# First chunk of a fused block on Trainium2: first tiles centred on VectorE and scaled on ScalarE, weights by single blocks, first up blocks by token halves

## The chip, the cores and the metric

One core of one Trainium2 chip runs the kernel. The metric is the device time of one execution in microseconds; the number that counts is the median of several executions. TensorE (PE in the profile, with its weight loads as PEld), VectorE (DVE), ScalarE (ACT), GpSimd (POOL) and the queue of SyncE (SP, its transfers as SPq) each work through their own list in program order, and meet only through semaphores.

## What is computed

For 8192 rows `x` of 256 numbers, everything in float32:

```
xn  = layernorm(x)                                   # no weights
D   = clip(slope of the counts over the first 1024 numbers of xn, 1, 2)
x1  = real(ifft(fft(xn) * filter(D)))                # a 256x256 circulant
cor = golay_correct(x1 @ W_el + b_el > 0) @ W_le + b_le
ffn = gelu(xn @ w1 + b1) @ w2 + b2                   # 256 -> 1024 -> 256
out = x + x1 + cor + ffn
```

## The kernel before

**Tiles.** The rows are cut into 16 chunks of 512 tokens. In a chunk the feed-forward part is 8 *up* blocks of 128 hidden units (line 964) and 8 *down* blocks (lines 982, 987). Each float32 operand is split into a high part that TensorE reads at full rate and a rest, so every product is three: high x high, low x high, high x low. An up block is thus 6 matmuls of 512 columns into one of the two PSUM banks `p_h[:, m % 2]`; ScalarE turns it into `h` by Gelu (line 446), then into `h_hi` (line 454), and VectorE makes `h_lo` (line 633). An up block `m` may start when the Gelu of block `m - 2` has emptied its bank (`gelu_done`), and the Gelu of block `m` wants `h_lo` of block `m - 2` (`h_lo_done`).

**Start.** SyncE loads the four row tiles of chunk 0 in three pieces (first tile, second tile, last two), then the identity matrix for transposes, the weights `w1` in pieces of 2, 2 and 4 blocks with other inputs between, and so on. VectorE takes the statistics of two tiles at a time (lines 824 and 830), GpSimd makes the inverse root (line 361, `rstd_done`), VectorE normalises with subtract and multiply in one instruction (line 817), TensorE transposes four 128x128 blocks for two tiles (line 1139, into one bank of `p_s`), ScalarE copies that bank to `xT_hi` (line 518, `t0_hi`), and VectorE makes `xT_lo` (line 839, `t0_lo`). Ahead of all this TensorE does 12 matmuls on zeros (line 1132). The parts of `w1` are copied to `w1_hi` by ScalarE (line 507) and to `w1_lo` by VectorE (line 804).

**Order in chunk 0.** It is written out by hand on each engine. TensorE: the transposes of both halves; up block 0 by token halves (256 columns) and up blocks 1 to 3 whole; then down and up in turn, with three small sums over partitions for `D` (line 1126), the circulant (line 1110, after down 5) and the latent weights (line 1119, after down 6) between. The sum that gives `D` (`logged` to `dim_made`) stands after down 1. From it VectorE makes `angle` (lines 880 to 883), GpSimd runs 12 small instructions up to `filt_w` (line 395), and ScalarE makes `basis_w` (line 549), which the circulant reads. ScalarE's list at the start:

```
w1_part_hi(0)
for g in range(2):
    act.wait_ge(t0_done, g + 1)
    nc.scalar.copy(half_tokens(xT_hi[0], g), half_bank(g)).then_inc(t0_hi, 1)
w1_part_hi(1)
act.wait_ge(small_in, 16)
gelu(0, 0, first=True)
hidden_hi(0, 0, first=True)
w2_part_hi(0)
gelu(0, 1, first=True)
```

**Later chunks** run one pattern, in a loop over pairs of chunks. The change leaves them alone.

Of the kernel before, what the change touches and what calls it, by code (L numbers as in the profile page):

```python
# [7 lines left out]
ALU = mybir.AluOpType  # L8
# [3 lines left out]
P = 128  # L12
TOKENS, E, HID, LAT, SYN = 2 * 4096, 256, 1024, 24, 12
TILES = TOKENS // P
CT = 4
CTOK = CT * P
# [6 lines left out]
W1_PARTS = ((0, 2), (2, 4), (4, 6), (6, MB))  # L23
W1_LOADS = ((0, 2), (2, 4), (4, MB))
# [40 lines left out]
def build(nc, x, xt, small, latent, w1, w2, ident, consts, basis, out):  # L65
    ctx = ExitStack()
    with ctx:
# [109 lines left out]
        id_in, con_in, basis_in, small_in = sem("id_in"), sem("con_in"), sem("basis_in"), sem("small_in")  # L177
# [13 lines left out]
        xn0_done, t0_done, t0_hi, t0_lo = sem("xn0_done"), sem("t0_done"), sem("t0_hi"), sem("t0_lo")  # L191
# [52 lines left out]
        def _(sp):  # L244
# [163 lines left out]
        def _(act):  # L408
# [117 lines left out]
            w1_part_hi(2)  # L526
# [3 lines left out]
            w1_part_hi(3)  # L530
# [46 lines left out]
        def _(dve):  # L577
# [235 lines left out]
            def normalise(g):  # L813

                dve.wait_ge(rstd_done, g + 1)
                for j in range(g * HALF, (g + 1) * HALF):
                    last = nc.vector.tensor_scalar(xn0[:, j, :], x_sb[0][:, j, :], mv[0][:, j, 0:1],  # L817
                                                   row_nums[0][:, 1, j:j + 1], ALU.subtract, ALU.mult)
                last.then_inc(xn0_done, 1)


# [5 lines left out]
            aggregate(0, range(HALF))  # L827
            dve.wait_ge(x_in[0], 16)
# [19 lines left out]
            w1_part_lo(1)  # L848
# [26 lines left out]
            w1_part_lo(3)  # L875
# [60 lines left out]
        def _(pe):  # L936
            mm = nc.tensor.matmul

            def up(c, par, m, first=False):

                if m == 0 and not first:

                    pe.wait_ge(t_lo, c)
                for n, (m0, _) in enumerate(W1_PARTS):
                    if first and m == m0:

                        pe.wait_ge(*((w1_hi_ready, 1) if n == 0 else (w1_ready, n + 1)))
                if not (first and m < 2):

                    pe.wait_ge(gelu_done, MB * c + m - 1)  # L950

                groups = 2 if first and m == 0 else 1
                for g in range(groups):
                    tok = slice(g * CTOK // groups, (g + 1) * CTOK // groups)
                    n = 0
                    for w, xp in ((w1_hi, xT_hi), (w1_lo, xT_hi), (w1_hi, xT_lo)):
                        if groups == 2:

                            if w is w1_lo and g == 0:
                                pe.wait_ge(w1_ready, 1)  # L960
                            elif w is w1_hi:
                                pe.wait_ge(t0_hi if xp is xT_hi else t0_lo, g + 1)
                        for k in range(KB):
                            last = mm(p_h[:, m % 2, tok], w[:, k, m * P:(m + 1) * P], xp[par][:, k, tok],  # L964
                                      start=(n == 0), stop=(n == 3 * KB - 1))
                            n += 1
                last.then_inc(up_done, 1)
# [165 lines left out]
            pe.wait_ge(id_in, 16)  # L1133
            for g in range(2):

                pe.wait_ge(xn0_done, g + 1)
                for k in range(KB):
                    for j in range(HALF):
                        last = nc.tensor.transpose(half_bank(g)[:, k, j * P:(j + 1) * P],  # L1139
                                                   xn0[:, g * HALF + j, k * P:(k + 1) * P], id_sb[:])  # L1140
                last.then_inc(t0_done, 1)

            pe.wait_ge(pool_set, 3)
            for m in range(LOOK):
# [3 lines left out]
            for m in range(MB):  # L1148
# [3 lines left out]
                if m == 1:  # L1152
# [16 lines left out]
def constants():  # L1169
# [50 lines left out]
    return np.eye(P, dtype=f4), con, basis  # L1220
# [47 lines left out]
```

## Time and profile before

| what | value |
|---|---|
| median of 3 runs | 407.75 us (407.51 to 407.8) |
| the profiled execution | 407.3 us, of which the span of the trace is 405.5 us |
| busy in the span | PE 99%, PEld 81%, DVE 74%, ACT 55%, POOL 21% |
| granted TensorE clock | 1.0 of full in every slice |
| chain that ended last | 97% PE |

The span runs from the first to the last instruction of the trace, and 1.8 us of the execution lie around it. All positions below are microseconds from the start of the span. A matmul's busy time contains its pipeline, so the pace of TensorE is read from the starts of the weight loads, which follow one another without overlap of their starts.

### The profile page before, as it was taken

What the parts mean: (1) busy time and instruction counts of PE and PEld (TensorE: products, weight loads), DVE (VectorE), ACT (ScalarE), POOL (GpSimd) and SP (SyncE); (2) the same over time, 40 slices, a digit from 0 to 9 for tenths busy, and PEclk for the clock granted to TensorE, in tenths of its full rate; (3) what the DMA queues carried; (4) which work ended last, traced back from release to release, by engine and by line L of the source; (5) the groups of instructions that cost most, each with busy time, mean ns of one, the idle gap of its engine ahead of it and who ended that gap; (6) DMA issues with size and microseconds to landing.
All of it is one profiled execution on the core that took longest, in us unless ns stands there. A gap on an engine that the chain in (4) does not pass through costs nothing.

```text
span 405.5 us, 5548 instructions
## 1 busy us (share of the span) xinstructions
PE 400.7 (99%) x1774; PEld 329.1 (81%) x1774; DVE 298.7 (74%) x512; ACT 223.3 (55%) x333; POOL 87.2 (21%) x102
## 2 busy tenths in 40 slices
PE   8999999999999999999999999999999999999997
PEld 3888888888888888888888888888888888888886
DVE  5879985878658795677957788476974868757656
ACT  3967556557354664537545474554736556365561
POOL 3142421313003131121313013131121312113000
PEclk9999999999999999999999999999999999999999
DMA  6554333213333213333123332023333031111011
GB/s 187 218 158 156 104 103 106 63 42 104 103 104 98 44 65 103 104 103 97 46 64 104 103 104 90 26 91 103 104 103 78 40 89 53 54 52 52 2 52 52
DMA packets 15307, 35.75 MB, mean 88 GB/s; under 512 B 5440, under 2 KB 6592, under 8 KB 15296
## 3 DMA queue, kind: packets, MB, share of 16 engines
q1 hardware_dynamic: 15152, 35.49, 27.4%
q10 hardware_dynamic: 144, 0.13, 0.1%
q8 instruction: 5, 0.08, 0.1%
q14 instruction: 6, 0.05, 0.0%
HBM read 27.17 MB, written 8.45 MB: 88 GB/s over the span
## 4 chain that ended last, share of the span: by engine, by line
PE 97%; DMA 1%; DVE 1%; POOL 0%; SPq 0%; issue 0%
PE p_h L964 43%; PE p_f L982 28%; PE p_f L987 14%; PE p_s L1030 5%; PE p_l L1017 4%; PE p_s L1038 2%; DMA x_sb<-x 1%; PE p_f L997 0%; SPq L248 0%; DVE stats L830 0%; POOL row_nums L361 0%; DVE rows_sb L817 0%; PE p_g L1006 0%; PE p_l L1006 0%; PE p_s L1139 0%
## 5 line engine op out<-in xcount | busy, mean ns | idle before, releaser
L446 ACT ACTIVATE h<-p_h,small_sb 128x512 f32<-128x512 f32 x128 | 88.2, 689 | 139.4 <-PE p_h L964 138.9
L633 DVE TENSOR_TENSOR h_lo<-h,h_hi 128x512 fp32r<-128x512 f32 x128 | 102.9, 804 | 69.2 <-ACT h_hi L454 69.2
L982 PE MATMUL p_f<-h_hi,w_hi 128*128 128x512 f32 x252 | 98.3, 390 | 0.0
L982 PE MATMUL p_f<-h_hi,w_lo 128*128 128x512 f32 x252 | 98.1, 389 | 0.0
L369 POOL TENSOR_TENSOR uv<-xn 128x512 f32<-128x512 f32 x30 | 59.3, 1996 | 126.0 <-DVE xn L618 126.0
L454 ACT CAST h_hi<-h 128x512 fp32r<-128x512 f32 x128 | 79.5, 621 | 5.8
L964 PE MATMUL p_h<-xT_hi,w_hi 128*128 128x512 f32 (+1 forms) x258 | 79.4, 389 | 0.0
L964 PE MATMUL p_h<-xT_lo,w_hi 128*128 128x512 f32 (+1 forms) x258 | 79.2, 388 | 0.0
L964 PE MATMUL p_h<-xT_hi,w_lo 128*128 128x512 f32 (+1 forms) x258 | 79.0, 387 | 0.0
L987 PE MATMUL p_f<-h_lo,w_hi 128*128 128x512 f32 x252 | 77.6, 389 | 0.0
L964 PEld LDWEIGHTS p_h<-xT_lo,w_hi 128*128 128x128 f32 x258 | 48.3, 188 | 10.3 <-DVE xT_lo L839 0.2
L964 PEld LDWEIGHTS p_h<-xT_hi,w_lo 128*128 128x128 f32 x258 | 48.3, 188 | 9.9
L964 PEld LDWEIGHTS p_h<-xT_hi,w_hi 128*128 128x128 f32 x258 | 48.0, 188 | 9.6
L982 PEld LDWEIGHTS p_f<-h_hi,w_hi 128*128 128x128 f32 x252 | 47.3, 188 | 10.0 <-issue 0.2
L987 PEld LDWEIGHTS p_f<-h_lo,w_hi 128*128 128x128 f32 x252 | 47.3, 188 | 9.9
L982 PEld LDWEIGHTS p_f<-h_hi,w_lo 128*128 128x128 f32 x252 | 47.3, 188 | 9.7
L356 POOL TENSOR_TENSOR var_eps<-mv,eps 128x4 f32<-128x4 f32 (+1 forms) x17 | 3.9, 227 | 153.3 <-DVE mv L596 153.3
L676 DVE SCALAR_TENSOR_TENSOR xt_sb<-p_f,bias,xt_sb 128x512 f32 (+1 forms) x30 | 21.1, 745 | 11.7 <-PE p_f L987 11.7
L416 ACT CAST xT_hi<-xn 128x1024 fp32r<-128x1024 f32 x15 | 15.8, 1054 | 19.8 <-DVE xn L618 19.8
L613 DVE TENSOR_TENSOR xn<-xt_sb,rows_sb 128x1024 f32<-128x1024 f32 x15 | 18.4, 1224 | 11.0 <-DMA rows_sb<-rows_dram 11.0
L628 DVE TENSOR_TENSOR uv_lo<-uv,uv_hi 128x1024 fp32r<-128x1024 f32 x16 | 19.3, 1203 | 3.3 <-ACT uv_hi L423 3.3
L591 DVE BATCH_NORM_STATS2 stats<-x_sb 128x6 f32<-128x256 f32 x60 | 21.0, 412 | 0.0
(127 smaller groups left out, 325.2 us busy)
## 6 DMA issues: line engine op xcount, KB each, us to landing
xt_sb<-xt SPq DMA_DIRECT2D x16, 512.0 KB, 5.3
x_sb<-x SPq DMA_DIRECT2D x15, 512.0 KB, 4.6
rows_sb<-rows_dram SPq DMA_DIRECT2D x15, 512.0 KB, 4.4
out<-xt_sb SPq DMA_DIRECT2D x15, 512.0 KB, 2.8
xt_sb<-w SPq DMA_DIRECT2D x3, 512.0 KB, 7.5
xt_sb<-w SPq DMA_DIRECT2D x2, 256.0 KB, 4.5
x_sb<-x SPq DMA_DIRECT2D x2, 128.0 KB, 2.1
x_sb<-x SPq DMA_DIRECT2D x1, 256.0 KB, 3.2
```

The lines of the kernel that those rows point to most:

```text
L369: nc.gpsimd.tensor_tensor(uv[:, k, :], xn[:, 0, :], xn[:, 1, :], op).then_inc(turned, 1)
L446: nc.scalar.activation(h[m % 2][:], p_h[:, m % 2, :], ACT.Gelu, bias=small_sb[:, S_B1 + m:S_B1 + m + 1]).then_inc(gelu_done, 1)
L454: nc.scalar.copy(h_hi[m % HR][:], h[m % 2][:]).then_inc(h_hi_done, 1)
L591: last = nc.vector.bn_stats(stats[:, j, :], x_sb[par][:, j, :])
L613: nc.vector.tensor_tensor(xn[:, :, :], columns(c), to_halves(rows_sb[par][:, 0, :]), ALU.subtract).then_inc(centred, 1)
L628: nc.vector.tensor_tensor(uv_lo[:, :, :], uv[:, :, :], uv_hi[:, :, :].bitcast(F32), ALU.subtract).then_inc(u_lo, 1)
L633: nc.vector.tensor_tensor(h_lo[m % HR][:], h[m % 2][:], h_hi[m % HR][:].bitcast(F32), ALU.subtract).then_inc(h_lo_done, 1)
L676: nc.vector.scalar_tensor_tensor(out=xc, in0=p_f[:, k, :], scalar=bias[:, k:k + 1], in1=xc, op0=ALU.add, op1=ALU.add).then_inc(ffn_added, 1)
L964: last = mm(p_h[:, m % 2, tok], w[:, k, m * P:(m + 1) * P], xp[par][:, k, tok], start=(n == 0), stop=(n == 3 * KB - 1))
L982: mm(p_f[:, a, :], w[:, m, a * HF:(a + 1) * HF], h_hi[r][:], start=(m == 0 and w is w2_hi), stop=False, skip_group_check=True)
L987: last = mm(p_f[:, a, :], w2_hi[:, m, a * HF:(a + 1) * HF], h_lo[r][:], start=False, stop=(m == MB - 1), skip_group_check=True)
L1030: last = mm(p_s[:, k, :], w[:, k, :], xp[:, k, :], start=(n == 0), stop=False, skip_group_check=True)
```

## The change

The identity matrix is no longer loaded: GpSimd makes it from `ones` with one affine_select, ahead of its four zeroing memsets. `w1` arrives and is split in parts of 1, 1, 2, 2 and 2 blocks (loads of 1, 1, 2 and 4). For the first two tiles VectorE only subtracts the mean, before it takes the statistics of the other two, and ScalarE multiplies by the inverse root. TensorE transposes tile by tile instead of column half by column half. Up blocks 0 and 1 are both done by token halves, in both banks of `p_h` at once; their first products for the first half stand ahead of the transposes of the second half. `up_done`, which releases the Gelu of blocks 0 and 1, comes with the last two pairs of matmuls. On VectorE the statistics of chunk 1 go ahead of `h_lo` of block 1; on TensorE the sum that gives `D` goes from behind down 1 to behind down 2.

```diff
-W1_PARTS = ((0, 2), (2, 4), (4, 6), (6, MB))
-W1_LOADS = ((0, 2), (2, 4), (4, MB))
+W1_PARTS = ((0, 1), (1, 2), (2, 4), (4, 6), (6, MB))
+W1_LOADS = ((0, 1), (1, 2), (2, 4), (4, MB))
...
-            sp.dma_start(id_sb[:], ident).then_inc(id_in, 16)
+            sp.dma_start(small_sb[:], small).then_inc(small_in, 16)
             load_w1(0)
-            sp.dma_start(small_sb[:], small).then_inc(small_in, 16)
             load_w1(1)
+            load_w1(2)
             sp.dma_start(con[:], consts).then_inc(con_in, 16)
             load_w2(0)
             load_x(1)
-            load_w1(2)
+            load_w1(3)
...
+            pool.wait_ge(pool_set, 3)
+
+            nc.gpsimd.affine_select(out=id_sb[:], in_=ones[:], pattern=[[1, P]], base=0, channel_multiplier=-1,
+                                    compare_op=ALU.is_equal, fill=0.0).then_inc(id_made, 1)
             for q in range(2):
                 nc.gpsimd.memset(cw[q][:].bitcast(F32), 0.0).then_inc(cw_set, 1)
                 nc.gpsimd.memset(le2[q][:].bitcast(F32), 0.0).then_inc(le_set, 1)
-            pool.wait_ge(pool_set, 3)
...
+            act.wait_ge(rstd_done, 1)
+            for j in range(HALF):
+                act.wait_ge(centred0, j + 1)
+                nc.scalar.mul(xn0[:, j, :], xn0[:, j, :], row_nums[0][:, 1, j:j + 1]).then_inc(scaled0, 1)
             w1_part_hi(0)
+            w1_part_hi(1)
             for g in range(2):
                 act.wait_ge(t0_done, g + 1)
                 nc.scalar.copy(half_tokens(xT_hi[0], g), half_bank(g)).then_inc(t0_hi, 1)
-            w1_part_hi(1)
+            w1_part_hi(2)
...
+            dve.wait_ge(stat_done, 1)
+            for j in range(HALF):
+                nc.vector.tensor_scalar(xn0[:, j, :], x_sb[0][:, j, :], mv[0][:, j, 0:1], None,
+                                        ALU.subtract).then_inc(centred0, 1)
             dve.wait_ge(x_in[0], 16)
             for j in range(HALF, CT):
                 last = nc.vector.bn_stats(stats[:, j, :], x_sb[0][:, j, :])
             last.then_inc(stats_made, 1)
             dve.wait_ge(stats_made, 2)
             aggregate(0, range(HALF, CT))
-            for g in range(2):
-                normalise(g)
             w1_part_lo(0)
+            dve.wait_ge(rstd_done, 2)
+            for j in range(HALF, CT):
+                nc.vector.tensor_scalar(xn0[:, j, :], x_sb[0][:, j, :], mv[0][:, j, 0:1], row_nums[0][:, 1, j:j + 1],
+                                        ALU.subtract, ALU.mult).then_inc(xn0_done, 1)
             for g in range(2):
                 dve.wait_ge(t0_hi, g + 1)
...
+                if g == 0:
+                    w1_part_lo(1)
...
-            w1_part_lo(2)
-            hidden_lo(0, 1)
+            w1_part_lo(3)
             statistics(1, 1)
             dve.wait_ge(stats_made, 3)
             aggregate(1)
+            hidden_lo(0, 1)
             hidden_lo(0, 2)
...
+            def first_ups():
+
+                turn_rows(0, scaled0)
+                pe.wait_ge(t0_hi, 1)
+                for m in range(2):
+                    pe.wait_ge(w1_hi_ready, m + 1)
+                    half_up(m, 0, (0,))
+                turn_rows(1, xn0_done)
+                pe.wait_ge(w1_ready, 1)
+                half_up(0, 0, (1,))
+                pe.wait_ge(t0_lo, 1)
+                half_up(0, 0, (2,))
+                half_up(1, 0, (2,), last_term=1)
+                pe.wait_ge(w1_ready, 2)
+                half_up(1, 0, (1,), last_term=1)
+                pe.wait_ge(t0_hi, 2)
+                half_up(0, 1, (0, 1))
+                half_up(1, 1, (0, 1))
+                pe.wait_ge(t0_lo, 2)
+                half_up(0, 1, (2,)).then_inc(up_done, 1)
+                half_up(1, 1, (2,)).then_inc(up_done, 1)
...
-            for m in range(LOOK):
+            first_ups()
+            for m in range(2, LOOK):
                 up(0, 0, m, first=True)
...
-                if m == 1:
+                if m == 2:
                     summed_over(16, 1, fr_d[:, 0:1], logged, dim_made)
```

`half_up(m, g, terms)` issues, for each of its terms (0 high x high, 1 low x high, 2 high x low), two matmuls of 256 columns into token half `g` of bank `m`. `turn_rows(g, ready)` issues four transposes, two for each tile as the tile becomes ready. Up block 2 still waits for the Gelu of block 0, and up block 3 for that of block 1.

## Rows read from the trace of the kernel before

**Rows 1.** The page, busy time, share of the span and number of instructions by engine.
```profile
PE 400.7 (99%) x1774; PEld 329.1 (81%) x1774; DVE 298.7 (74%) x512; ACT 223.3 (55%) x333; POOL 87.2 (21%) x102
```

**Rows 2.** Timeline, 0 to 8.6 us: start, length, engine, line, operation, [idle before].
```profile
1.19 5.30 PE L1132 MATMUL p_f<-idle 128*128 128x512 bf16 x12 [1.19 <-DVE idle L578]
4.42 0.71 POOL L361 TENSOR_TENSOR row_nums<-var_eps,minus_half 128x2 f32<-128x2 f32 x1
...
6.62 0.42 PEld L1139 LDWEIGHTS p_s<-id_sb,rows_sb 128*128 128x128 f32 x4 [1.04 <-issue]
...
7.09 0.62 ACT L507 CAST w_hi<-xt_sb 128x512 fp32r<-128x512 f32 x1 [4.86 <-DMA xt_sb<-w]
...
7.62 0.58 ACT L518 CAST xT_hi<-p_s 128x512 fp32r<-128x512 f32 x1
...
7.89 0.66 PE L1139 MATMUL p_s<-id_sb,rows_sb 128*128 128x128 f32 x4 [0.61 <-DVE rows_sb L817]
...
8.31 0.30 PEld L964 LDWEIGHTS p_h<-xT_hi,w_hi 128*128 128x128 f32 x2
...
8.59 0.59 ACT L518 CAST xT_hi<-p_s 128x512 fp32r<-128x512 f32 x1 [0.39 <-PE p_s L1139]
```

**Rows 3.** Timeline, 9.3 to 13.2 us, the up blocks 0 to 3 and their Gelus.
```profile
9.32 0.30 PEld L964 LDWEIGHTS p_h<-xT_hi,w_hi 128*128 128x128 f32 x2
...
9.55 0.30 PEld L964 LDWEIGHTS p_h<-xT_hi,w_lo 128*128 128x128 f32 x2
...
9.95 0.30 PEld L964 LDWEIGHTS p_h<-xT_lo,w_hi 128*128 128x128 f32 x2
...
10.56 0.69 ACT L446 ACTIVATE h<-p_h,small_sb 128x512 f32<-128x512 f32 x1 [0.87 <-PE p_h L964]
...
11.46 0.41 PEld L964 LDWEIGHTS p_h<-xT_hi,w_hi 128*128 128x128 f32 x2
...
12.33 0.68 ACT L446 ACTIVATE h<-p_h,small_sb 128x512 f32<-128x512 f32 x1
...
13.16 0.30 PEld L964 LDWEIGHTS p_h<-xT_hi,w_hi 128*128 128x128 f32 x2
```

**Rows 4.** DMA issues of the first 30 us: KB each, median us to landing.
```profile
xt_sb<-w SPq DMA_DIRECT2D x2, 256.0 KB, 4.5
...
x_sb<-x SPq DMA_DIRECT2D x2, 128.0 KB, 2.1
...
small_sb<-small SPq DMA_DIRECT2D x1, 30.0 KB, 4.2
```

**Rows 5.** ScalarE by form, first 35 us: busy us, mean ns.
```profile
L556 ACT ACTIVATE le_h<-le_t 128x256 fp32r<-128x256 f32 x1 | 0.4, 427 | 0.0
```

**Rows 6.** Timeline, GpSimd at the start.
```profile
0.80 0.20 POOL L339 MEMSET ones<- 128x128 f32 x1
...
4.15 0.20 POOL L356 TENSOR_TENSOR var_eps<-mv,eps 128x2 f32<-128x2 f32 x1 [2.15 <-DVE mv L596]
```

**Rows 7.** The page, GpSimd's costliest group: busy, mean ns, idle before.
```profile
L369 POOL TENSOR_TENSOR uv<-xn 128x512 f32<-128x512 f32 x30 | 59.3, 1996 | 126.0 <-DVE xn L618 126.0
```

**Rows 8.** Timeline, the chain from the sum for D to the circulant.
```profile
18.79 0.42 PEld L1126 LDWEIGHTS p_g<-fr_d,ones 128*128 128x128 f32 x2
...
20.31 0.15 DVE L880 TENSOR_SCALAR fr_d<-p_g 128x1 f32<-128x1 f32 x1
...
26.01 0.19 POOL L395 TENSOR_TENSOR filt_w<-series 128x2 f32<-128x2 f32 x1
...
27.50 0.69 ACT L549 ACTIVATE basis_w<-basis_sb,filt_w 128x128 f32<-128x128 f32 x2
...
28.55 0.65 PEld L1110 LDWEIGHTS p_l<-basis_w,basis_sb 128*128 128x128 f32 x4
```

**Rows 9.** Timeline, the statistics of chunk 1 and the Gelu of block 3.
```profile
15.42 1.40 DVE L591 BATCH_NORM_STATS2 stats<-x_sb 128x6 f32<-128x256 f32 x4
...
16.37 0.68 ACT L446 ACTIVATE h<-p_h,small_sb 128x512 f32<-128x512 f32 x1
```

More of the change, by code:

```diff
@@ L62, with build @@
 S_END = S_WEL + KB * LAT
-def build(nc, x, xt, small, latent, w1, w2, ident, consts, basis, out):
+def build(nc, x, xt, small, latent, w1, w2, consts, basis, out):
     ctx = ExitStack()
@@ L176, in build @@
         w2_in = [sem(f"w2_in{i}") for i in range(len(W2_LOADS))]
-        id_in, con_in, basis_in, small_in = sem("id_in"), sem("con_in"), sem("basis_in"), sem("small_in")
+        id_made, con_in, basis_in, small_in = sem("id_made"), sem("con_in"), sem("basis_in"), sem("small_in")
         latent_in, stored = sem("latent_in"), sem("stored")
@@ L190, in build @@
         veps_done, rstd_done, mean_done = sem("veps_done"), sem("rstd_done"), sem("mean_done")
[L191 removed]
+        centred0, scaled0, xn0_done, t0_done, t0_hi, t0_lo = sem("centred0"), sem("scaled0"), sem("xn0_done"), sem("t0_done"), sem("t0_hi"), sem("t0_lo")
         fr_taken, xc0_made = sem("fr_taken"), sem("xc0_made")
@@ L525, in _ @@
             hidden_hi(0, 1, first=True)
-            w1_part_hi(2)
+            w1_part_hi(3)
             gelu(0, 2, first=True)
@@ L529, in _ @@
             w2_part_hi(1)
-            w1_part_hi(3)
+            w1_part_hi(4)
             gelu(0, 3, first=True)
@@ L811, in w2_part_lo @@
                                         ALU.subtract).then_inc(w2_ready, 1)
[L813 to L819, printed above, removed]
             for j in range(HALF):
@@ L847, in _ @@
             values = fr_v[:, :].unsqueeze(1).broadcast_to(table)
-            w1_part_lo(1)
+            w1_part_lo(2)
             first_rows = p_s[:, :, :].rearrange("p g (a t) -> p (g a) t", t=P)[:, :, 0]
@@ L874, in _ @@
                                     ALU.add).then_inc(logged, 1)
-            w1_part_lo(3)
+            w1_part_lo(4)
             w2_part_lo(1)
@@ L945, in up @@
                     if first and m == m0:
[L947 to L966, printed above, removed]
@@ L967, in up @@
-                last.then_inc(up_done, 1)
+                        pe.wait_ge(w1_ready, n + 1)
+                pe.wait_ge(gelu_done, MB * c + m - 1)
+                n = 0
+                for w, xp in ((w1_hi, xT_hi), (w1_lo, xT_hi), (w1_hi, xT_lo)):
+                    for k in range(KB):
+                        last = mm(p_h[:, m % 2, :], w[:, k, m * P:(m + 1) * P], xp[par][:, k, :],
+                                  start=(n == 0), stop=(n == 3 * KB - 1))
+                        n += 1
@@ new lines, in up, with turn_rows, half_up @@
+                last.then_inc(up_done, 1)
+            def turn_rows(g, ready):
+                for j in range(HALF):
+                    pe.wait_ge(ready, j + 1)
+                    for k in range(KB):
+                        last = nc.tensor.transpose(half_bank(g)[:, k, j * P:(j + 1) * P],
+                                                   xn0[:, g * HALF + j, k * P:(k + 1) * P], id_sb[:])
+                last.then_inc(t0_done, 1)
+            def half_up(m, g, terms, last_term=2):
+                tok = slice(g * GTOK, (g + 1) * GTOK)
+                for n in terms:
+                    w, xp = ((w1_hi, xT_hi), (w1_lo, xT_hi), (w1_hi, xT_lo))[n]
+                    for k in range(KB):
+                        last = mm(p_h[:, m, tok], w[:, k, m * P:(m + 1) * P], xp[0][:, k, tok],
+                                  start=(n == 0 and k == 0), stop=(n == last_term and k == KB - 1), skip_group_check=True)
+                return last
@@ L1132, in _ @@
                 mm(p_f[:, 0, :], idle[:, 0:P], idle[:], start=True, stop=True)
[L1133 to L1141, printed above, removed]
+            pe.wait_ge(id_made, 1)
             pe.wait_ge(pool_set, 3)
-            for m in range(LOOK):
+            first_ups()
+            for m in range(2, LOOK):
                 up(0, 0, m, first=True)
@@ L1219, in constants @@
     assert a.sum(axis=1).min() >= 4
-    return np.eye(P, dtype=f4), con, basis
+    return con, basis
 def layouts(inputs):
@@ L1255 @@
     arrays = {name: np.ascontiguousarray(a) for name, a in layouts(inputs).items()}
-    for name, a in zip(("ident", "consts", "basis"), constants()):
+    for name, a in zip(("consts", "basis"), constants()):
         arrays[name] = a
```

## The prediction

> **What bounds the kernel now.** I read the page first. TensorE is busy in 99% of the span and no other engine in more than 81% [rows 1], and the chain that ended last runs over TensorE for 97% of it. So the time is what TensorE has to do plus the time in which it can't go on, and the change takes no real work from it: the same products, some of them in pieces of 256 columns. What can move is the head, so I then read the timeline of the first 15 us, engine by engine, and there the starts of the weight loads, because a matmul's busy time hides small gaps.
>
> The head before reads like this. TensorE's matmuls on zeros end at 6.49 [rows 2]. The first transposes start at 6.62; ScalarE could take them at about 7.3, but it is on the first piece of `w1`, which landed at 7.09, and copies `xT_hi` from 7.62 to 8.20. The first up matmul loads at 8.31 [rows 2]. From there pairs of 256 columns go at 0.23 us a pair (9.32 to 9.55), so the six pairs of block 0 need 1.38; the last pair loads at 9.95, so they took until 10.18, and 0.49 of it was waiting for `xT_lo` and the second half [rows 3]. Then TensorE goes on without a pause: block 2 loads at 11.46, block 3 at 13.16, one block and one small sum (1.70) later [rows 3]. The Gelu of block 0 runs 10.56 to 11.25, so its bank is free just before block 2 wants it at 11.46; the Gelu of block 1 ends at 13.01, again just before 13.16 [rows 3]. After this I find no wait of TensorE worth counting in the first 40 us. The measure for the change is therefore one number: when blocks 2 and 3 load, against 11.46 and 13.16. I call the shift of block 3 **s**.
>
> **When the first up matmul loads (T).** Three things can set it.
>
> - *The rows.* The inverse root is there at 5.13 [rows 2]. The two subtractions fit into VectorE's pause before the second statistics, and cost nothing there. ScalarE waits for nothing else then, and its scaling of 128x256 is nearest to an ACTIVATE of that shape, 0.43 [rows 5]; two, overlapping, or at worst one after the other, end between 5.9 and 6.1.
> - *The matmuls on zeros* are in front of the transposes in TensorE's list and unchanged. The last ends at 6.49 with its pipeline; the next load may overlap it a little, so the transposes start at 6.3 to 6.5 instead of 6.62. In the second half ScalarE's copy began 0.70 after the transposes (7.89 to 8.59) [rows 2], so this path lets the copy begin at 7.0 to 7.2.
> - *The weights.* ScalarE now has parts 0 and 1 of `w1` ahead of this copy. The two are the bytes of the old first piece, but in two transfers; the first keeps its place in SyncE's list, the second is issued 0.47 later, in the place in which the small inputs were. The old piece took 4.5 from issue to landing, the small inputs 4.2, the first row tile, with an empty queue, 2.1 [rows 4]. The old issue was thus at 2.59 and the second one's is near 3.06; it lands between 5.2 (2.1 later) and 7.3 (4.2 later). With half the bytes of the old piece and the identity's 64 KB gone from ahead of it, I take 6.8, nearer to the late end, since what lies in front of it in the queue is the same. Half a copy (about 0.27, as 7.09 to 7.62 is 0.53 for the whole) brings the copy of `xT_hi` to 7.07.
>
> Both last paths meet near 7.1. Then 0.58 for the copy and 0.11 to the load, as from 7.62 to 8.31: T = 7.8, with 7.7 and 8.3 as ends. That is 0.5 earlier than before, and it is what the change gains.
>
> **What follows T.** Four half matmuls (0.46), then the second half's transposes. Their loads took 0.42 for the first half, and they were already through before T in the old order, so this is work that goes from a pause of TensorE into its busy time. The second copy of `xT_hi` begins 0.46 + 0.70 after T and is seen at T + 1.85. Until then TensorE has 0.46 + 0.44 + four pairs (0.92) = 1.82: no pause. VectorE has the two `xT_lo` in time: the first runs from about T to T + 0.7 and is wanted at T + 1.13, the second ends near T + 2.5 and is wanted at T + 2.77. The parts of `w1_lo` lie between them, with 0.4 or more to spare. So both blocks are issued at T + 0.46 + 0.44 + 10 pairs (2.30) = T + 3.2. With T = 7.8 this is 11.0, where the old order needed until about 11.5. So far 0.5 gained.
>
> **Where the gain goes.** Blocks 0 and 1 now end together. `up_done` comes first with the last but one pair, which loads at T + 2.77. Before, the Gelu of block 0 started 0.61 after the load of that block's last pair (9.95 to 10.56) [rows 3]. So it starts at T + 3.38 = 11.18, lasts 0.69, and block 2, which waits for it to empty the bank, loads 0.10 later, at T + 4.17 = 11.97. TensorE stands for 0.95 us, where it stood for nothing. Block 2 loads at 11.97 instead of 11.46: 0.5 late. For block 3 the Gelu of block 1 counts. Between the two Gelus ScalarE has `h_hi` of block 0 and a part of `w2`, 1.77 from start to start (10.56 to 12.33) [rows 3], and no idle time, so it starts at T + 5.15 and ends at T + 5.83, and block 3 loads at T + 5.94 = 13.74. By TensorE's own path it would be 11.97 + 1.70 = 13.67. Against 13.16 this is s = T - 7.22 = **+0.58**, from +0.48 (T = 7.7) to +1.08 (T = 8.3).
>
> **The rest of chunk 0.** The whole order moves by s; I looked for places where it moves by more.
>
> - *Statistics of chunk 1 ahead of `h_lo` of block 1.* Four instructions of 1.40 in all and four small ones [rows 9], with the second ones I count 1.8. Behind that `h_lo` waits the Gelu of block 3, at 16.37 before [rows 9]; it now starts near 17.9 and ends at 18.6. It is needed by up block 5, which now loads in the old place of the sum, 18.79 + s [rows 8]. The Gelu of block 4, behind three copies on ScalarE, ends near 21.7; it is needed by up block 6, two blocks (2.72) and a sum (0.34) after block 5, 21.8 + s. Costs 0, with 0.6 to spare; without that cover up to 0.9 us.
> - *The sum for D, one up and one down block later.* It loads at 21.5 + s instead of 18.79, but VectorE got to its result only at 20.31 [rows 8] and will at 22.1 + s, 1.8 later. So `filt_w` moves from 26.20 to 28.0 + s, and `basis_w` from 27.50 to 28.05 + s. Each of its two halves takes some 0.35; the circulant loads at 28.55 + s [rows 8] and its second half 0.28 later. They are ready at 28.4 and 28.75. It just fits: 0 to 0.1. Here VectorE and ScalarE stand in line behind the wait (`w2_lo`, `h_lo` of blocks 4 and 5, the Gelus of 6 and 7), but each of these is needed over 1 us later than it then comes.
> - *GpSimd.* No row shows an affine_select. Below it is bounded by the 128x128 memset, 0.20, above by a two-input operation on four times the elements, 2.0 [rows 6, 7]. GpSimd was idle for 2.15 before its first statistics at 4.15 [rows 6], so both ends cost nothing. I take 0.5. The identity is wanted at 6.3.
> - *One transfer less* (identity) saves nothing on the path beyond what stands above.
>
> The sum: -0.5 for the earlier start, +0.44 for transposes that move into busy time, -0.49 for the pauses of block 0 that go, +0.95 for the new pause, and some 0.15 where block 3 is held by ScalarE and in rounding: +0.55 to +0.6. The profiled execution was 407.3, its span 405.5, so I expect 407.9 for a profiled one; on the median of the runs, 407.75, it gives **408.35**.
>
> **One rule against the trace.** GpSimd's instructions of the start, each the first of its kind, took 0.1 to 0.7 us, the longest the power at 4.42 [rows 2, 6]. The Trainium skill (GPSIMD Engine Reference, Instruction dispatch) says that the first call of a freshly loaded kernel pays about 6 us to bring in its code. By that page, if it held for affine_select, the result would be near 411; the trace shows no such pause for the other operations.
>
> **The rivals.**
>
> 1. *Weights land late.* Two transfers, each with its own finish, land at 7.3 or after; T is 8.3 or more and s = +1.1, time 408.85. For it: the small inputs issued in that slot took 4.2 [rows 4]. Against it: less lies in the queue ahead.
> 2. *The chain for D loses its cover.* If the sum's result comes 0.5 later than I think, the circulant waits as long and everything behind it: s = +1.1 to +1.6, time 409.1. For it: 0.1 us of slack.
> 3. *The first copy is early enough (the other side).* It decides at T = 7.22. If the zeros ended by 6.0 and the weights landed by 6.1, the copy would begin at 6.4, T = 7.1 and s = -0.1; at T = 6.4, which needs the rows' path to end at 5.7, it would be 0.8 faster, 406.95. Against it: the 12 matmuls on zeros end at 6.49 and are not touched [rows 2]. The new pause can vanish too, if the next bank is seen free sooner than by the rows: then 407.4.
> 4. *GpSimd's first affine_select is slow.* It delays the first inverse root one for one beyond 2.15. A stall of 6 us in its place would put T near 11 and the time at 411.3.
> 5. *Nothing changes*: gain and pause cancel within 0.2, 407.75.
>
> **How the numbers follow.** The forecast (s from 0.4 to 0.8) has 0.55, the late weights 0.13, the lost cover 0.09, the other side 0.09, the slow affine_select 0.03, no change 0.11. A difference of 0.2%, 0.8 us, is about what a measurement of this kernel can tell from none. Of the forecast's own chance a tenth lies above 0.8, and of the first two rivals nearly all; of the other side half is faster by more than 0.2%. So slower 0.30, same 0.65, faster 0.05. The range, 407.5 to 409.1, leaves out the slow affine_select, the far part of the lost cover and most of the other side, together under 0.2; the forecast's own is 408.15 to 408.55.
>
> **What would show it.** In the profile after: transposes from 6.3 to 6.5 and the first up load at 7.7 to 8.3 (right), TensorE without a pause up to about 11, then one of 0.8 to 1.0 before block 2 that ends with the Gelu of block 0; block 3 near 13.75; the circulant near 29.15. The prediction is wrong if that pause is absent or small, if the first load is before 7.2 or after 8.6, if affine_select is longer than 2.1, or if there is a second pause between 16 and 32 us.

## The result, and the profile after

The changed kernel takes 409.81 us (median of 6 runs), the kernel before 407.59 on the same chips. The ratio is 1.0056, with a 95% interval of 1.0043 to 1.0069: 2.2 to 2.3 us slower. The forecast was 408.35 with a range to 409.1. Its account of the head held, and a second loss of 2 us was missed. Its point lay on the right side, though its chances did not favour it: "slower" had 0.30 and "same" 0.65. The missed loss is a pause between 16 and 32 us, which the prediction had named as a sign of being wrong.

First the page of the changed kernel: busy time by engine, and the chain that ended last.

```profile
span 407.9 us, 5566 instructions
...
PE 400.2 (98%) x1780; PEld 329.3 (81%) x1780; DVE 298.7 (73%) x513; ACT 224.2 (55%) x336; POOL 90.0 (22%) x103
...
PE 95%; POOL 2%; DMA 1%; ACT 1%; SPq 0%; issue 0%; DVE 0%; ACTq 0%
```

Against [rows 1] TensorE's busy time is the same within 0.5 us, and the span is 2.4 us longer, so the difference is TensorE standing. GpSimd has 2.8 us more busy time for one instruction more, and it now has 2% of the chain. Both are the trace of what follows.

The timeline of the head, the lines that answer to [rows 2, 3]:

```profile
6.07 0.54 PEld L972 LDWEIGHTS p_s<-id_sb,rows_sb 128*128 128x128 f32 x4 [0.98 <-issue]
...
6.52 0.71 ACT L510 CAST w_hi<-xt_sb 128x256 fp32r<-128x256 f32 x2 [0.17 <-DMA xt_sb<-w]
...
7.14 0.58 ACT L526 CAST xT_hi<-p_s 128x512 fp32r<-128x512 f32 x1
...
7.77 0.53 PEld L982 LDWEIGHTS p_h<-xT_hi,w_hi 128*128 128x128 f32 x4 [1.16 <-ACT xT_hi L526]
...
10.59 0.55 PEld L982 LDWEIGHTS p_h<-xT_lo,w_hi 128*128 128x128 f32 x4
...
11.21 0.69 ACT L449 ACTIVATE h<-p_h,small_sb 128x512 f32<-128x512 f32 x1 [1.11 <-PE p_h L982]
...
12.01 0.30 PEld L962 LDWEIGHTS p_h<-xT_hi,w_hi 128*128 128x128 f32 x2 [0.87 <-issue]
...
13.71 0.30 PEld L962 LDWEIGHTS p_h<-xT_hi,w_hi 128*128 128x128 f32 x2
```

The first up matmul loads at 7.77 (8.31 before), block 2 at 12.01 (11.46), after a pause of 0.87 that ends with the Gelu of block 0, and block 3 at 13.71 (13.16). The head is 0.54 us ahead at its start and 0.55 behind at its end.

Now the second loss. The waits of the weight loads in the first 60 us (us in total, times, longest), of which only this one stands behind block 3:

```profile
PEld p_l L1149 <- ACT basis_w L557: 2.0, 1, 2.0
```

And the timeline of what the circulant waited for, to be read against [rows 8]:

```profile
22.64 0.16 DVE L888 TENSOR_SCALAR fr_d<-p_g 128x1 f32<-128x1 f32 x1 [1.61 <-PE p_g L1165]
...
26.75 0.53 POOL L394 TENSOR_TENSOR halves<-halves,quads 128x8 f32<-128x8 f32 x1
27.36 1.06 POOL L395 TENSOR_TENSOR series<-halves,powers 128x4 f32<-128x4 f32 x1
28.49 1.19 POOL L396 TENSOR_TENSOR series<-series,halves 128x4 f32<-128x4 f32 x1
29.76 0.52 POOL L397 TENSOR_TENSOR series<-series,weighted 128x4 f32<-128x4 f32 x1
30.36 0.19 POOL L398 TENSOR_TENSOR filt_w<-series 128x2 f32<-128x2 f32 x1
...
31.09 0.59 PEld L1149 LDWEIGHTS p_l<-basis_w,basis_sb 128*128 128x128 f32 x4 [2.00 <-ACT basis_w L557]
```

VectorE reads the sum at 22.64, as forecast (22.1 + s). But `filt_w` is ready at 30.55 and not at 28.6: the GpSimd chain from `angle` on took 7.2 us, where it took 5.2 before. Beside the slow instructions VectorE did this:

```profile
25.93 1.29 DVE L641 TENSOR_TENSOR h_lo<-h,h_hi 128x512 fp32r<-128x512 f32 x2
27.14 1.22 DVE L621 TENSOR_TENSOR xn<-xt_sb,rows_sb 128x1024 f32<-128x1024 f32 x1
28.39 1.23 DVE L626 TENSOR_TENSOR xn<-xn,rows_sb 128x1024 f32<-128x1024 f32 x1
29.54 0.68 DVE L641 TENSOR_TENSOR h_lo<-h,h_hi 128x512 fp32r<-128x512 f32 x1
```

Put the ends side by side: VectorE's four end at 27.22 (the second of the two), 28.36, 29.62 and 30.22; GpSimd's four slow ones at 27.28, 28.42, 29.68 and 30.28. Each GpSimd instruction on four or eight numbers ends 0.06 us after a VectorE instruction with two operands in SBUF. So it looks as if it had not been working that long but standing; the third experiment tests that.

### The profile page after: what moved, and what is told of

The parts are those of the page before. It is cut to its first block, busy times and chain, and to the rows that moved or that the text cites. A ratio compares the mean times of both kernels' runs of the same rounds, so it can differ in the third digit from the quotient of the medians.

```text
span 407.9 us, 5566 instructions
## 1 busy us (share of the span) xinstructions
PE 400.2 (98%) x1780; PEld 329.3 (81%) x1780; DVE 298.7 (73%) x513; ACT 224.2 (55%) x336; POOL 90.0 (22%) x103
## 4 chain that ended last, share of the span: by engine, by line
PE 95%; POOL 2%; DMA 1%; ACT 1%; SPq 0%; issue 0%; DVE 0%; ACTq 0%
PE p_h L962 42%; PE p_f L1021 27%; PE p_f L1026 14%; PE p_s L1069 5%; PE p_l L1056 4%; PE p_s L1077 2%; DMA xt_sb<-w 1%; PE p_h L982 1%; PE p_f L1036 0%; SPq L248 0%; POOL series L396 0%; POOL powers L385 0%; POOL series L395 0%; PE p_l L1149 0%; PE p_g L1045 0%
## 5 line engine op out<-in xcount | busy, mean ns | idle before, releaser
L962 PE MATMUL p_h<-xT_hi,w_hi 128*128 128x512 f32 x252 | 78.0, 391 | 0.7 <-ACT h L449 0.7
L962 PE MATMUL p_h<-xT_lo,w_hi 128*128 128x512 f32 x252 | 77.6, 389 | 0.0
L962 PE MATMUL p_h<-xT_hi,w_lo 128*128 128x512 f32 x252 | 77.6, 389 | 0.0
L962 PEld LDWEIGHTS p_h<-xT_hi,w_hi 128*128 128x128 f32 x252 | 47.0, 188 | 10.4 <-issue 0.9
L962 PEld LDWEIGHTS p_h<-xT_lo,w_hi 128*128 128x128 f32 x252 | 47.3, 188 | 9.9
L962 PEld LDWEIGHTS p_h<-xT_hi,w_lo 128*128 128x128 f32 x252 | 47.3, 188 | 9.9
L684 DVE SCALAR_TENSOR_TENSOR xt_sb<-p_f,bias,xt_sb 128x512 f32 (+1 forms) x30 | 21.1, 746 | 11.9 <-PE p_f L1026 11.7
```

The costliest lines, as they stand in the source:

```text
L684: nc.vector.scalar_tensor_tensor(out=xc, in0=p_f[:, k, :], scalar=bias[:, k:k + 1], in1=xc, op0=ALU.add, op1=ALU.add).then_inc(ffn_added, 1)
L962: last = mm(p_h[:, m % 2, :], w[:, k, m * P:(m + 1) * P], xp[par][:, k, :], start=(n == 0), stop=(n == 3 * KB - 1))
```

## The experiments

All times are given against runs of the kernel before on the same chip, as a ratio with its 95% interval; its median there was 407.2 to 407.3 us.

**The sum back in its place.** Only this is undone in the changed kernel:

```diff
-                if m == 2:
+                if m == 1:
                     summed_over(16, 1, fr_d[:, 0:1], logged, dim_made)
```

> The changed kernel with one thing undone: the sum that gives D stands again behind down block 1 on TensorE. Theory A (the moved sum costs the 2.0 us pause ahead of the circulant, since the twelve GpSimd instructions start later and also run beside VectorE's centring and scaling of chunk 1): the chain on GpSimd starts near 21.5 and takes 5 to 5.5 us, the pause before the circulant is gone, and only the shift of the head, +0.55, is left: 0.5 to 0.7 us above the kernel before, about 1.7 us below the changed one. Theory B (the late VectorE and ScalarE order, with the statistics of chunk 1 ahead of h_lo of block 1, causes the pause; the sum's place is not what matters): the pause stays over 1 us and the time stays within 0.5 us of the changed kernel.

Measured 407.83, ratio 1.0026 (1.0013 to 1.004), by medians 0.6 us above the kernel before. The chain starts at 21.29 and ends at 26.45, and nothing waits for `basis_w` any more. Theory A holds, B falls. One thing was not expected, a new wait of 0.58 us ahead of the latent weights:

```profile
PEld p_g L1158 <- ACT c_f L561: 0.6, 1, 0.6
```

What sets this wait shows when the traces are laid side by side. VectorE starts to centre chunk 1 when its row numbers arrive, and the latent weights' product loads 3.88 or 3.89 us after that start, in the kernel before (26.54 and 30.43), here (27.29 and 31.17) and in all five kernels below that have a wait for `c_f`. The start is 0.75 us later here: the row numbers leave 0.14 later, and the rest is that their transfers took longer in this execution.

**The sum alone,** moved in the kernel before (`if m == 1:` to `if m == 2:`).

> The kernel before with only the sum for D moved behind down block 2. Theory A: the sum is read at about 22.05 instead of 20.31, the GpSimd chain starts near 22.7, its last four instructions fall beside VectorE's centring and scaling from 26.5 on and are stretched as in the changed kernel; filt_w is ready near 29.7 instead of 26.2, and TensorE pauses 1.5 to 2.2 us before the circulant: 1.3 to 2.0 us above the kernel before. Theory C (the GpSimd instructions merely vary from run to run; the move costs the slack of 1.8 minus 1.7): 0 to 0.4 us above.

Measured 409.04, ratio 1.0046 (1.0033 to 1.0059): 1.8 us above, from one moved matmul pair, and the wait for `basis_w` is 2.0. Its GpSimd rows repeat those of the changed kernel at other times (1.06, 1.18 and 0.52 us from 26.64, 27.77 and 29.04, under VectorE's centring, scaling and `h_lo` from 26.42), so this is no scatter. Theory C falls.

**VectorE stands aside.** The changed kernel, with one wait more:

```diff
             hidden_lo(0, 6)
+            dve.wait_ge(filt_made, 1)
             centre(1, 1)
```

> The changed kernel, with VectorE waiting for filt_w before it centres chunk 1, so that no two-input VectorE instruction runs beside the end of the GpSimd chain. Theory A: the last four GpSimd instructions (0.53, 1.06, 1.19 and 0.52 us in the changed kernel) shrink to 0.2 each, or 0.7 where something else ran beside them before; the chain ends near 28.5 instead of 30.55; the pause before the circulant falls from 2.0 to under 0.3, and a new one of up to 1 us may come further on, since centring now starts later: 0.5 to 1.8 us below the changed kernel. Theory C: their durations stay, and the time rises by 1 us or more, since centring waits.

Measured 409.17, ratio 1.0047 (1.0033 to 1.0062). By medians this is 0.6 us below the changed kernel, but each against the kernel before on its own chips they are 1.95 and 2.22 us slower, and the intervals overlap: a gain in time is not shown. What the experiment shows is in the timeline, the same instructions:

```profile
26.72 0.53 POOL L394 TENSOR_TENSOR halves<-halves,quads 128x8 f32<-128x8 f32 x1
27.32 0.20 POOL L395 TENSOR_TENSOR series<-halves,powers 128x4 f32<-128x4 f32 x1
27.60 0.20 POOL L396 TENSOR_TENSOR series<-series,halves 128x4 f32<-128x4 f32 x1
27.88 0.20 POOL L397 TENSOR_TENSOR series<-series,weighted 128x4 f32<-128x4 f32 x1
28.16 0.19 POOL L398 TENSOR_TENSOR filt_w<-series 128x2 f32<-128x2 f32 x1
```

1.06, 1.19 and 0.52 have become 0.20 each; the first, still beside an `h_lo`, stays at 0.53. `filt_w` is ready 2.2 us earlier although the chain began at the same time, and the circulant doesn't wait. The time does not fall by as much because centring is now late, at 28.38, and behind it `xT_hi` and `c_f`, for which the latent weights wait 1.4 (up to 1 us was expected).

**Half of the move,** the sum behind up block 5, in the kernel before and in the changed one (the call goes behind `up(0, 0, m + LOOK, first=True)` with `if m == 1:`).

> The kernel before with the sum for D one up block later than before, behind up block 5: half of the move of the change. Theory A (a threshold: the sum costs nothing until the GpSimd chain slides under VectorE's centring of chunk 1): VectorE reads the sum near 20.7, the chain ends between 26.6 and 27.5, the circulant does not wait, and the time is within 0.2 us of the kernel before. Rival G (the cost grows with the distance moved, 1.8 us for two places): 0.6 to 1.2 us above the kernel before.

Measured 407.37, ratio 1.0000 (0.9991 to 1.0008). No cost in the median, but the two other marks of theory A failed: in the profiled execution (407.59) the row numbers of chunk 1 arrived early, VectorE centred from 25.34, and the chain was stretched to 28.48, 7.3 us long, with 0.7 of wait before the circulant. Part of that came back, since the 0.2 us of wait before chunk 1's first down block were gone; the block loads at 39.91, 0.24 later than in the kernel before. So the place is at the edge, not safe: what the chain meets depends on when the row numbers arrive.

> The changed kernel with the sum for D behind up block 5 instead of behind down block 2. Theory A: no wait before the circulant beyond 0.3 us, time within 0.3 us of e1_sum_back, so 0.3 to 0.9 us above the kernel before. Rival G: half of the 2 us pause stays, 1.3 us or more above the kernel before.

Measured 408.12, ratio 1.0013 (1.0004 to 1.0022). The chain took 5.1 us and the circulant didn't wait; the wait for `c_f` was 1.1, with centring from 27.89. On the time theory A holds in both kernels and rival G falls; that the circulant doesn't wait holds here only. What counts is not how far the sum moves but what the chain then meets.

**The head alone,** with the statistics of chunk 1 behind `h_lo` of block 1 again and the sum back:

```diff
             w1_part_lo(3)
+            hidden_lo(0, 1)
             statistics(1, 1)
             dve.wait_ge(stats_made, 3)
             aggregate(1)
-            hidden_lo(0, 1)
```

> The changed kernel with both moves behind the head undone: the sum for D and the statistics of chunk 1 in their old places. What is left is the head alone (centring, scaling, single blocks, token halves, identity from GpSimd). Theory A: block 2 loads 4.2 us after the first up matmul, the wait for c_f is 0 to 0.6, and the time is 0.3 to 0.7 us above the kernel before. Rival F (the statistics' move helps, since the row numbers of chunk 1 leave earlier): e1_sum_back is faster than this by 0.2 us or more.

Measured 408.01, ratio 1.0017 (1.0002 to 1.0033), and 0.2 us of median apart from the kernel with only the sum back, whose interval overlaps. First up matmul 7.93, block 2 at 12.16: 4.23 apart, as in the changed kernel (4.24) and with the sum back (4.21). Whether the statistics' move helps is not told apart by this pair's times. The traces say how much it could: in the five kernels with the statistics in the place of the change the row numbers leave 11.7 us after the first up matmul loads, in the four with the old place 11.9 to 12.0.

**Where the 0.6 us near 30 comes from.** The statistics still earlier, in the time in which VectorE had nothing to do:

```diff
             nc.vector.tensor_reduce(fr_s[:, 0, :], fr_a[:], AX.X, ALU.add).then_inc(part_sums, 1)
+            statistics(1, 1)
+            dve.wait_ge(stats_made, 3)
+            aggregate(1)
             hidden_lo(0, 0)
...
             w1_part_lo(3)
-            statistics(1, 1)
-            dve.wait_ge(stats_made, 3)
-            aggregate(1)
             hidden_lo(0, 1)
```

> As e1_sum_back, with the statistics of chunk 1 still earlier on VectorE, ahead of h_lo of block 0, where it had 1.1 us without work. Theory H (what the kernels with the sum in its old place lose near 30 us is the wait for the row numbers of chunk 1: statistics, root, two transfers, centring, xT_hi and, behind it on ScalarE, c_f): the row numbers leave about 3 us earlier, TensorE does not wait for c_f (0.3 to 1.1 us in e1_sum_back, e5_sum_stats_back and e10_sum_between), and the time is 0.2 to 0.6 us below e1_sum_back, so within 0.4 us of the kernel before. Rival D (VectorE has no room there: h_lo of block 0, w2_lo and the Gelu of block 2 come late): a wait of 0.5 us or more between 14 and 20 us, and no gain against e1_sum_back.

Measured 407.98, ratio 1.002 (1.001 to 1.0029). The mechanism is as theory H has it, and the time is not: the row numbers leave at 15.74 instead of 19.16, the latent weights don't wait, and the profile lists no wait of TensorE's weight loads behind block 2. But the kernel is not faster than with the sum back, and 0.8 us by medians above the kernel before where at most 0.4 was expected. For this one execution the profile shows a head that began late.

```profile
8.06 0.53 PEld L982 LDWEIGHTS p_h<-xT_hi,w_hi 128*128 128x128 f32 x4 [1.53 <-ACT xT_hi L526]
...
12.29 0.30 PEld L962 LDWEIGHTS p_h<-xT_hi,w_hi 128*128 128x128 f32 x2 [0.87 <-issue]
```

In this one block 2 is 0.62 us behind its time with the sum back (11.67), because the first up matmul loads at 8.06 and not at 7.46. A gap that is given back elsewhere and a start that scatters by 0.6 us are of one size here. Why the median of 11 runs is no lower, one profile doesn't show. It does show the head's own loss without the wait for `c_f`: block 2 is 0.83 late, chunk 1's first down block 0.64 and the span 0.7.

**Three banks.** Does the pause before block 2 cost what it seems to? In chunk 0 the up blocks go round three banks, so block 2 waits for nothing and block 3 for the Gelu of block 0:

```diff
+        def up_bank(m, first):
+            if first and m in (2, 5):
+                return p_l[:, :]
+            return p_h[:, (0, 1, 0, 0, 1, 0, 0, 1)[m] if first else m % 2, :]
...
-                pe.wait_ge(gelu_done, MB * c + m - 1)
+                if not first:
+                    pe.wait_ge(gelu_done, MB * c + m - 1)
+                elif m > 2:
+                    pe.wait_ge(gelu_done, m - 2)
```

First with the sum back and nothing else:

> As e1_sum_back, and in chunk 0 the up blocks use three banks (blocks 2 and 5 in the bank that the circulant uses later), so that block 2 waits for no Gelu and block 3 only for that of block 0. Theory A (the head loses its gain because both first blocks end together and block 2 waits for the Gelu of block 0): the pause of 0.9 us before block 2 is gone, block 2 loads near 11.1 and block 3 near 12.8, against 11.46 and 13.16 before; if nothing behind takes it back the time is 0.3 to 0.4 us below the kernel before, and about 0.9 below e1_sum_back. Rival D (ScalarE, without idle time until 20, is the real bound of the stretch): the pause moves to up block 4 or 5 and the time stays within 0.3 us of e1_sum_back.

Measured 408.07, ratio 1.0026 (1.0016 to 1.0035). Block 2 loads 3.3 us after the first up matmul and block 3 4.9, so the pause is gone. But at the sum for D, TensorE now waits 0.99 us, until 19.57, for VectorE, which has not yet made its input:

```profile
19.57 0.30 PEld L1174 LDWEIGHTS p_g<-fr_d,ones 128*128 128x128 f32 x2 [0.99 <-DVE fr_d L887]
```

Rival D, with VectorE in place of ScalarE. Three more kernels tried to clear the way. With the statistics back and `c_f` ahead of `xT_hi` on ScalarE:

> As e4_third_bank, with the statistics of chunk 1 in their old place and c_f ahead of xT_hi of chunk 1 on ScalarE. In e4_third_bank the gain of the head was lost to a 1.0 us wait of the sum for D on VectorE and 0.3 us for c_f. Theory A: both waits are gone or under 0.3 together, block 3 loads about 4.8 us after the first up matmul instead of 5.9, and the time is 0.2 to 0.6 us below the kernel before. Rival D (ScalarE and VectorE bound the stretch from 10 to 20 us, or the transfer of the row numbers the one up to 31): a wait of 0.5 us or more stands elsewhere before 35 us, and the time is no more than 0.2 us below the kernel before.

Measured 408.43, ratio 1.0025 (1.0016 to 1.0034): the wait before the sum stayed, at 1.0, that for `c_f` went, and the swap brought waits of 0.3 for `cw`, the latent weights that VectorE writes, and 0.7 before chunk 1's first down block. The swap alone, which shows what that wait is, in the kernel before:

> A control: the kernel before with one swap in ScalarE's list, the copy c_f of the circulant ahead of the 128x1024 copy xT_hi of chunk 1. In the kernel before TensorE loads the latent weights' product 0.06 us after c_f is there, so this chain has no reserve but does not bind. Theory A: no change beyond 0.2 us. Rival E (c_f already costs TensorE time in the kernel before): 0.3 us or more below the kernel before.

Measured 407.81, ratio 1.0013 (1.0004 to 1.0022), 0.5 us slower. Neither theory. The copy to `xT_hi`, which now stands behind `c_f`, is on a path of its own: `xT_lo` starts at 30.67 (30.14 before), and from there VectorE goes through its list, in both kernels with only one pause, 0.55 for ScalarE's `uv_hi`, until it has emptied the bank that chunk 1's first down block needs. The last instructions of that stretch, first in the kernel before, then here:

```profile
38.17 1.38 DVE L676 SCALAR_TENSOR_TENSOR xt_sb<-p_f,bias,xt_sb 128x512 f32<-128x512 f32 x2
```

```profile
38.72 1.38 DVE L676 SCALAR_TENSOR_TENSOR xt_sb<-p_f,bias,xt_sb 128x512 f32<-128x512 f32 x2
```

And the down block's first weight load, again before and here:

```profile
39.67 0.19 PEld L982 LDWEIGHTS p_f<-h_hi,w_hi 128*128 128x128 f32 x1 [0.23 <-issue]
```

```profile
40.21 0.18 PEld L982 LDWEIGHTS p_f<-h_hi,w_hi 128*128 128x128 f32 x1 [0.68 <-ACT h_hi L454]
```

The adding ends at 39.55 and 40.10, the block loads 0.12 and 0.11 us later. So in the kernel before TensorE waits here already, for 0.23 us, and the 0.53 by which `xT_lo` is late comes through whole. Row numbers that come late do the same: in the kernels that wait for `c_f`, this block loads 13.1 us after VectorE starts to centre, as in the kernel before. (The profile names `h_hi`, a copy that ended long before.)

> As e8_bank_stats_cf, and ScalarE copies the second single block of w1 only after the first copy of xT_hi. The first up matmul waited for this block's landing and copy. Theory A: it loads 0.1 to 0.5 us earlier, near 7.5, and the time is 0.1 to 0.3 us below e8_bank_stats_cf if nothing later takes it back. Rival D: same time as e8_bank_stats_cf within 0.1, the earlier start being lost before 35 us.

Measured 408.33, ratio 1.0023 (1.0014 to 1.0032), no lower. The first up matmul loads at 7.79 and not near 7.5, since `xT_hi` now waited 0.52 for the transposes. With the sum behind up block 5 instead, and ScalarE's order left alone:

> Third bank for chunk 0, statistics of chunk 1 in their old place, the sum for D behind up block 5, ScalarE's order as in the changed kernel. In the earlier third-bank kernels TensorE waited 0.95 us for the sum's input at 18 us. Theory A: that wait is gone. Rival D (the transfer of the row numbers of chunk 1, whose start hangs on VectorE and whose end releases xT_hi and behind it c_f, is the next bound): TensorE then waits 0.6 to 1.2 us for c_f near 30 us, and the time is within 0.3 us of the kernel before, though the head is 0.5 to 1 us ahead at block 3. If rival D fails the time is 0.4 to 1.0 us below the kernel before.

Measured 407.98, ratio 1.0013 (1.0002 to 1.0023). Block 3 is 0.4 us ahead of the kernel before; then TensorE waits 1.3 for `c_f`, as rival D says, and ends behind, by medians 0.7 us, more than the 0.3 that the rival allowed.

**Both together.** Statistics early and three banks, and, as one change more, `w2_lo` ahead of `h_lo` of block 0:

> e13_stats_early with three banks for the up blocks of chunk 0 and w2_lo ahead of h_lo of block 0 on VectorE. Theory A (the pause ahead of block 2 is the head's cost, and nothing behind takes the time back): block 3 loads 4.9 us after the first up matmul instead of 5.9, no later wait above 0.3 us, and the time is 0.7 to 1.0 us below e13_stats_early, so 0 to 0.3 us below the kernel before. Rival D (some other queue binds by then): a wait of 0.5 us or more between 14 and 41 us, and a time above the kernel before.

Measured 407.5, ratio 1.0 (0.9992 to 1.0009), the first version of the changed head that is not slower, 0.5 us below the one with early statistics and two banks, by medians on two chips; the intervals don't overlap. Theory A has the place of the cost right and expected more (0.7 to 1.0, and no wait above 0.3); rival D's wait is there, its time above the kernel before is not. Block 3 loads at 12.42, 4.92 after the first; then TensorE stands twice more, 0.2 before up block 4 and before that ahead of down block 0:

```profile
14.57 0.19 PEld L1030 LDWEIGHTS p_f<-h_hi,w_hi 128*128 128x128 f32 x1 [0.92 <-ACT h_hi L463]
```

The profile names `h_hi`, but that copy ended long before. The block also waits for `w2_lo`, which VectorE finished at 14.45, behind the statistics:

```profile
12.05 1.41 DVE L605 BATCH_NORM_STATS2 stats<-x_sb 128x6 f32<-128x256 f32 x4 [0.89 <-DMA x_sb<-x]
13.49 0.38 DVE L610 BATCH_NORM_AGGREGATE mv<-stats 128x2 f32<-128x6 f32 x4
13.79 0.66 DVE L824 TENSOR_TENSOR w_lo<-xt_sb,w_hi 128x512 fp32r<-128x512 f32 x1
```

> The same with the second single block of w1 copied behind the first copy of xT_hi. Theory A: the first up matmul loads near 7.5 instead of 7.6 to 8.1, and the time is another 0.1 to 0.4 us lower, 0.2 to 0.6 us below the kernel before. Rival D: no lower than e14_bank_stats_early.

Measured 407.38, ratio 1.0004 (0.9995 to 1.0013). The same, as rival D says. In the profiled execution the first up matmul loads at 7.98: the first row tiles came late, and VectorE centred from 4.66, where eight of the twelve profiled executions of this head have 4.12 to 4.26. No version tried beats the kernel before.

## Why the prediction was right about the head and wrong about the time

**When the first up matmul loads.** Forecast 7.8, with 7.7 to 8.3; it was 7.77, and 7.46 to 8.06 in the eleven other kernels with this head. Two paths were to meet near 7.1; in this execution the weights decided alone. Their copies ran 6.52 to 7.23, after 0.17 of waiting for the landing, and ScalarE took the bank at 7.14. The transposes were through at 6.85. They began at 6.07 (6.3 to 6.5 forecast), held by ScalarE's scaling, since the matmuls on zeros ended at 5.58, 0.9 us earlier than in the kernel before, the last ones at a quicker pace. That was luck: in the kernel with the head alone they ended at 6.54, and there the transposes held the copy. The scaling ended at 6.36, not by 6.1.

**What follows it.** Block 2 was forecast 4.17 after T and block 3 5.94; they came 4.24 and 5.94 after it. s was forecast +0.58 and was +0.55. What it costs at the end is shown less directly. With the later moves undone the kernel is 0.6 to 0.8 us slower than before, but both of those kernels wait for `c_f`, and chunk 1's first down block is late by as much as VectorE's centring (0.76 and 0.75, 0.93 and 0.91): their time is that of the late row numbers, whatever the head lost. Only the kernel with the statistics early shows the head's loss without that wait, 0.8 us by medians. Three banks remove the pause before block 2 each time (block 3 4.9 after T); with the statistics in either later place another queue takes the time back, and with the statistics early 0.5 us reach the end, though `w2_lo` was moved there too and its share is not told apart.

**Statistics of chunk 1.** Forecast at no cost, and no cost was seen. What I had overlooked is what hangs on them: root, two transfers, centring, scaling, `xT_hi`, and `c_f` behind it in ScalarE's list. In the kernel before, that chain ends 0.06 us before TensorE loads what needs it. When it is late or TensorE early, the latent weights wait 0.3 to 1.4 us. And the same chain goes on through `xT_lo` and VectorE's list to chunk 1's first down block, before which TensorE waits 0.2 us in the kernel before. A gain of the head had to pass both, and with ScalarE's order unchanged neither came earlier unless centring did.

**The sum for D, the step that failed.** "So `filt_w` moves from 26.20 to 28.0 + s" and "It just fits: 0 to 0.1". The 1.8 was right. The 5.2 us of the GpSimd chain was wrong: I took it from a trace in which VectorE had nothing to do for 0.65 us of that time and again from 25.60 on, and was not yet centring, and moved it into a stretch without such pauses. Measured 7.2, which gives the pause of 2.0 before the circulant. This was rival 2 in place and sign, at up to 1.6 us all told and with a chance of 0.09; it lacked the mechanism, and so the size. The trace of the kernel before had shown it: a GpSimd instruction of the same form took 0.2 or 0.7 us, by whether an `h_lo` ran beside it, as the rows of the two engines show.

```profile
23.58 0.68 DVE L633 TENSOR_TENSOR h_lo<-h,h_hi 128x512 fp32r<-128x512 f32 x1
23.67 0.65 POOL L389 TENSOR_TENSOR halves<-quads,powers 128x8 f32<-128x8 f32 x1
...
24.40 0.20 POOL L391 TENSOR_TENSOR halves<-halves,quads 128x8 f32<-128x8 f32 x1
24.68 0.20 POOL L392 TENSOR_TENSOR series<-halves,powers 128x4 f32<-128x4 f32 x1
24.91 0.69 DVE L633 TENSOR_TENSOR h_lo<-h,h_hi 128x512 fp32r<-128x512 f32 x1 [0.65 <-ACT h_hi L454]
24.96 0.70 POOL L393 TENSOR_TENSOR series<-series,halves 128x4 f32<-128x4 f32 x1
25.74 0.20 POOL L394 TENSOR_TENSOR series<-series,weighted 128x4 f32<-128x4 f32 x1
...
26.54 1.23 DVE L613 TENSOR_TENSOR xn<-xt_sb,rows_sb 128x1024 f32<-128x1024 f32 x1 [0.94 <-DMA rows_sb<-rows_dram]
```

`h_lo` ends at 24.26 and 25.60 and the long ones at 24.32 and 25.66, again 0.06 later.

The Trainium skill has the rule (GPSIMD Engine Reference, Key points): GpSimd shares its SBUF interfaces with VectorE and contends with VectorE instructions that have two SBUF inputs. The trace agrees, and is sharper: 1.06, 1.19 and 0.52 us beside them against 0.20 without. Of that page I had weighed the rule on first calls instead; the affine_select took 0.29 us.

**The sum.** +0.55 for the head and +2.0 for the circulant make 2.55; 0.23 came back before the first down block of chunk 1, since the changed kernel is so late there that VectorE has long emptied the bank. That block loads at 41.99 against 39.67, 2.3 later, and the span is 2.4 longer: nothing of note happens behind it. The shift of a version can be read at this place: +0.76 with the sum back (span +0.7), +0.64 with the statistics early (+0.7), +0.54 with `c_f` first in the kernel before (+0.5).

## What to carry to other kernels

A duration is only worth carrying to another place in the order together with what ran beside it: when a chain on GpSimd moves, read its instructions against VectorE's at the old place and at the new one. If two matmul groups are interleaved to start sooner, ask when the first of them ends, since that is what its reader and its bank wait for. In a kernel that is busy at 99%, list the chains that end just ahead of TensorE (here the Gelus of blocks 0 and 1, `basis_w` and `c_f`, all within 31 us) before claiming a gain from an earlier start; here what was gained stopped at the next one.

## What the runs showed of the hardware

- A GpSimd instruction on a few numbers (0.20 us by itself) stood until the VectorE instruction beside it ended, when that had two SBUF operands, and ended 0.06 us after it. Beside VectorE's statistics, which read one SBUF tensor, a GpSimd power on 128x2 took 0.73, and 0.70 with nothing beside it. Two SBUF operands are not the only case: beside the subtraction of the row means in the changed kernel (one tensor and one number per row, ends at 4.55) a GpSimd addition on 128x2 took 0.36 and ended at 4.61, against 0.20 with nothing beside it.
- The first up matmul of this head loaded between 7.46 and 8.06 us in twelve profiled executions, a scatter of the size of the effects that were looked for. What held it differed: the landing of the weights (with the statistics early, 0.18 and 0.26 us of waiting ahead of their copies), the transposes (the head alone, 0.24 ahead of the copy of the bank), or first row tiles that came late (three banks with the sum back, centring from 4.74).
- The two transfers that spread the row numbers of chunk 1 took 2.3 to 3.2 and 3.8 to 5.2 us for the same bytes.
